# Loading the inputs of the next step one step ahead in the inner attention (8 cores)

## What is computed

```python
def _layer(x, wqkv, qs, ksc, wo, lg, lb, w1, b1, w2, b2):
    h = shift_token(x)                 # upper half of the features comes from the token before
    qkv = h @ wqkv                     # 1024 -> 3 * 512
    q, k, v = to_heads(...)            # 8 heads of 64
    q = l2norm(q) * qs;  k = l2norm(k) * ksc
    q, k = rotary_xpos(q, k)           # q*cos*scale + rotate_half(q)*sin*scale; k with 1/scale
    o = local_attention(q, k, v)       # windows of 512: own and previous, masked, softmax
    x = x + o @ wo
    ...                                # then shift, layer norm, gated feed-forward
```

## Time and profile before

| what | us |
|---|---|
| median of 3 runs (lowest, highest) | 8637.81 (8518.31, 8813.91) |
| the profiled execution | 8547.56 |
| its span, on core 6, the slowest | 8545.7 |
| spans of the 8 cores | 8432.1 to 8545.7 |

### The profile page before, as it was taken

One profiled execution on the slowest core, in us unless ns is written; L12 is line 12 of the kernel. 1 busy time (PEld: TensorE's weight loads), 2 busy tenths in 40 slices (PEclk: granted clock), 3 DMA queues, 4 the chain that ended last, 5 costly groups with the idle time before them and its releaser, 6 DMA issues. The chain is left out here.

```text
span 8545.7 us, 72782 instructions; the slowest of 8 cores (8432.1 to 8545.7 us)
## 1 busy us (share of the span) xinstructions
PE 5767.5 (67%) x21696; PEld 2068.7 (24%) x21696; DVE 2308.5 (27%) x4472; ACT 2490.9 (29%) x4771; POOL 634.1 (7%) x944
## 2 busy tenths in 40 slices
PE   1139677777777557767758877957776749779853
PEld 0013121222122112212213333412222214334321
DVE  1101221221110333334321322224333321321347
ACT  0002556666767412222211111112222221111201
POOL 0010000000000000000011111110000001111100
PEclk7568788888989866667669989966666659889876
DMA  9982001110110241121156665631112146645643
GB/s 79 86 88 73 6 25 20 30 30 7 23 25 1 47 83 35 35 59 45 35 103 95 73 105 95 83 90 35 35 39 65 35 88 80 95 98 82 87 138 138
DMA packets 694032, 531.89 MB, mean 62 GB/s; under 512 B 426620, under 2 KB 560092, under 8 KB 693664
## 3 DMA queue, kind: packets, MB, share of 16 engines
q0 software_dynamic: 472720, 208.37, 23.0%
q1 hardware_dynamic: 220944, 318.86, 15.3%
HBM read 466.56 MB, written 176.19 MB: 75 GB/s over the span
## 5 line engine op out<-in xcount | busy, mean ns | idle before, releaser
L1341 PE MATMUL p_pb<-p_hn,p_w 128*128 128x512 bf16 (+1 forms) x5632 | 1250.1, 386 | 216.1 <-DVE p_hn L1257 148.3
L600 ACT ACTIVATE p_pt<-p_pss 128x512 bf16<-128x512 f32 (+3 forms) x2304 | 1168.4, 559 | 481.8 <-PE p_pss L368 288.7
L383 PE MATMUL p_psz<-p_pt,p_v 128*65 128x512 bf16 x2304 | 777.5, 422 | 183.9 <-DVE p_zt L496 103.2
L1341 PEld LDWEIGHTS p_pb<-p_hn,p_w 128*128 128x128 bf16 (+1 forms) x5632 | 557.2, 99 | 911.6 <-issue 269.8
L368 PE MATMUL p_pss<-p_qtb,p_kt 64*128 64x512 bf16 (+3 forms) x2304 | 556.2, 404 | 234.9 <-ACT p_pt L600 219.7
L1356 PE MATMUL p_pb<-p_h,p_w 128*128 128x512 bf16 (+1 forms) x2816 | 648.4, 385 | 27.3 <-DVE p_x L1280 19.3
L810 PE MATMUL p_pb<-p_xq,p_wqkv 128*128 128x512 bf16 x1024 | 282.1, 444 | 464.3 <-DMA p_xq<-xb 406.4
L1087 ACT ACTIVATE p_pt<-p_pb 128x128 bf16<-128x128 f32 (+1 forms) x960 | 367.4, 434 | 748.9 <-PE p_pb L870 747.7
L877 PE MATMUL p_pb<-p_pt,p_vr 128*65 128x512 bf16 x960 | 501.6, 630 | 107.3 <-DVE p_pt L1003 104.3
L1308 ACT ACTIVATE p_glu<-p_pb,p_bc 128x512 bf16<-128x512 f32 x352 | 241.9, 687 | 1097.1 <-PE p_pb L1341 1097.0
L1267 DVE SCALAR_TENSOR_TENSOR p_h<-p_pb,p_bc,p_glu 128x512 bf16<-128x512 f32 x352 | 264.4, 751 | 966.2 <-PE p_pb L1341 966.2
(11 more groups left out here) (158 smaller groups left out, 5299.2 us busy)
## 6 DMA issues: line engine op xcount, KB each, us to landing
p_w<-w POOLq DMA_DIRECT2D x336, 256.0 KB, 4.2
p_xf<-xf SPq DMA_DIRECT2D x16, 2048.0 KB, 15.3
xf<-p_x POOLq DMA_DIRECT2D x128, 256.0 KB, 5.1
xb<-p_x POOLq DMA_DIRECT2D x256, 128.0 KB, 4.4
p_hf<-xf SPq DMA_DIRECT2D x32, 1024.0 KB, 9.3
p_xr<-xf SPq DMA_DIRECT2D x16, 2048.0 KB, 9.4
xf<-p_x SPq DMA_DIRECT2D x128, 256.0 KB, 2.7
xf<-p_stage SPq DMA_DIRECT2D x32, 512.0 KB, 27.5
```

The source lines that it names most:

```text
L383: t.matmul(ps_z[ZBANK[h]][0:65, 0:512], v_bf[:, kt * 520 + g * 65:kt * 520 + g * 65 + 65], pt[GS % 8][:, 0:512], start=(kt == 0), stop=(kt ...
L600: s.activation(pt[GS % 8][:, off:512], ps_s[GS % 3][:, off:512], AF.Exp, scale=0.125).then_inc(sE.sem, 1)
L1341: inst = t.matmul(pb[bank + gi % 2][0:jw, :] if jw < 128 else pb[bank + gi % 2][:, :], w1buf[:, (seq % 4) * NC * 128 + kc * jw: (seq % 4) ...
```

## The change

`xq_in` and `tabs` become twice as large, and step `tb` uses the half `tb % 2`. Each half has its own semaphore. Step 0 loads its own inputs and those of step 1. Step `tb` (1 to 6) loads those of step `tb + 1`, after two waits for semaphore values that had been reached when the step before ended; step 7 loads only `xf_cur`. The load of `xf_cur` is still that of the own step, and comes behind the others. TensorE and DVE keep their waits, on the semaphore of their half; from step 1 on the value they wait for is that at the start of the step.

```diff
-    xq_in = en(nc.sbuf_tensor("p2_xq" + L, [128, NC * 512], BF16))
+    xq_in = en(nc.sbuf_tensor("p2_xq" + L, [128, 2 * NC * 512], BF16))
-    tabs = en(nc.sbuf_tensor("p2_tab" + L, [128, 4 * 512], F32))
+    tabs = en(nc.sbuf_tensor("p2_tab" + L, [128, 2 * 4 * 512], F32))
-    lxq = Ctr.get(en_sem, nc, "p2_lxq")
+    lxq2 = [Ctr.get(en_sem, nc, f"p2_lxq{i}") for i in range(2)]
-    ltb = Ctr.get(en_sem, nc, "p2_ltb")
+    ltb2 = [Ctr.get(en_sem, nc, f"p2_ltb{i}") for i in range(2)]
...
             @blk.sync
             def _(sy):
+                def load_tb(tbl):
+                    xo = (tbl % 2) * NC * 512
+                    to = (tbl % 2) * 4 * 512
+                    sy.dma_start(xq_in[:, xo:xo + 4 * 512].rearrange("p (c j) -> p c j", c=4),
+                                 xb_in[0:512, 1 + tbl * 512:1 + (tbl + 1) * 512]
+                                 .rearrange("(c p) j -> p c j", p=128)
+                                 ).then_inc(lxq2[tbl % 2].sem, 16)
...
+                    for i, tab in enumerate([tab_cs, tab_sn, tab_ci, tab_si]):
+                        sy.dma_start(tabs[:, to + i * 512:to + (i + 1) * 512],
+                                     tab[:, tbl * 512:(tbl + 1) * 512]
+                                     ).then_inc(ltb2[tbl % 2].sem, 16)
+                    ltb2[tbl % 2].val += 64
+
+                if tb == 0:
+                    load_tb(0)
+                if tb + 1 < NQB:
+                    if tb >= 1:
+                        sy.wait_ge(tV.sem, tV0)
+                        sy.wait_ge(vQ.sem, vQ0)
+                    load_tb(tb + 1)
                 sy.dma_start(xf_cur[:, :].rearrange("p (c j) -> p c j", c=NC),
...
             @blk.tensor
             def _(t):
-                t.wait_ge(lxq.sem, lxq0 + 32)
+                xo = (tb % 2) * NC * 512
+                t.wait_ge(lxq2[tb % 2].sem, lxq20[tb % 2] + (32 if tb == 0 else 0))
...
             @blk.vector
             def _(v):
-                v.wait_ge(ltb.sem, ltb0 + 64)
+                to = (tb % 2) * 4 * 512
+                v.wait_ge(ltb2[tb % 2].sem, ltb20[tb % 2] + (64 if tb == 0 else 0))
```

More of the change, by code:

```diff
@@ L758, in _p2_inner_attn @@
             msidx[u] = mpos.get(u, 0)
-        lxq0, lxf0, ltb0 = lxq.val, lxf.val, ltb.val
+        lxf0 = lxf.val
+        lxq20 = [c.val for c in lxq2]
+        ltb20 = [c.val for c in ltb2]
         tQ0, vQ0, tV0, vV0, sSq0 = tQ.val, vQ.val, tV.val, vV.val, sSq.val
@@ L772, in _ @@
             def _(sy):
[L773 to L781, removed]
+                def load_tb(tbl):
[5 more added lines that the diff above has]
+                                 ).then_inc(lxq2[tbl % 2].sem, 16)
+                    sy.dma_start(xq_in[:, xo + 4 * 512:xo + NC * 512]
+                                 .rearrange("p (c j) -> p c j", c=4),
+                                 xb_in[512:1024, 0 + tbl * 512:0 + (tbl + 1) * 512]
+                                 .rearrange("(c p) j -> p c j", p=128)
+                                 ).then_inc(lxq2[tbl % 2].sem, 16)
+                    lxq2[tbl % 2].val += 32
+                    for i, tab in enumerate([tab_cs, tab_sn, tab_ci, tab_si]):
[10 more added lines that the diff above has]
+                    load_tb(tb + 1)
                 sy.dma_start(xf_cur[:, :].rearrange("p (c j) -> p c j", c=NC),
@@ L784, in _ @@
                              .rearrange("(c p) j -> p c j", p=128)).then_inc(lxf.sem, 16)
-                lxq.val += 32
                 lxf.val += 16
-                ltb.val += 64
             @blk.gpsimd
@@ L811, in _ @@
                                         wqkv_bf[:, kc * 1536 + mc * 128:kc * 1536 + mc * 128 + 128],
-                                        xq_in[:, kc * 512:(kc + 1) * 512],
+                                        xq_in[:, xo + kc * 512:xo + (kc + 1) * 512],
                                         start=(kc == 0), stop=(kc == NC - 1))
@@ L820, in _ @@
                         inst = t.matmul(pb[2 + tt % 2][:, :],
-                                        xq_in[:, kc * 512 + tt * 128:kc * 512 + tt * 128 + 128],
+                                        xq_in[:, xo + kc * 512 + tt * 128:
+                                              xo + kc * 512 + tt * 128 + 128],
                                         wqkv_bf[:, kc * 1536 + 1024:kc * 1536 + 1536],
@@ L932, in _ @@
             def _(v):
-                v.wait_ge(ltb.sem, ltb0 + 64)
+                to = (tb % 2) * 4 * 512
+                v.wait_ge(ltb2[tb % 2].sem, ltb20[tb % 2] + (64 if tb == 0 else 0))
                 for i in range(4):
                     v.tensor_single_scalar(ctabs[:, i * 512:(i + 1) * 512],
-                                           tabs[:, i * 512:(i + 1) * 512],
+                                           tabs[:, to + i * 512:to + (i + 1) * 512],
                                            scol[:, i:i + 1], ALU.mult).then_inc(vch.sem, 1)
```

## The result

The changed kernel took 8387.86 us (median of 10 runs, lowest 8307.37), the kernel before 8541.16 us in 10 runs beside it (lowest 8453.84). The ratio is 0.978, with a 95% interval of 0.974 to 0.982: 189 us less, where 153 were forecast and the range was 8330 to 8530. That the two medians of all runs lie 153 us apart, exactly the forecast, is chance (see the part on the prediction).

The account below looks back on a forecast made before the run. The prediction took the serial path across each attention step boundary (stores, drain, barrier, loads, projection) as the bound on that stretch. Its sum, 97 - 1 + 48 + 9 = 153 us off 8547.6, gave 8395 us, range 8330 to 8530.

Parts of the forecast that it names:

- Order of the waits: Between attention steps: stores, drain, barrier, xq and table loads, projection, all serial; one 23.23 us pause is 15.2 drain, 8.1 load.
- Term 1: TensorE's wait for xq after the release, 6.9 us in each of 14 steps, goes: gain 97 less 1 us.
- term 2: The stop ahead of the 17th matmul, where DVE waits for the tables, shrinks in 14 steps: gain 48 us.
- term 3: TensorE's clock in the projection dips less once the stop is gone: gain 9 us, bounds 0 and 20.
- What is added: Extra issues, waits, later xf_cur load and drain at the attention steps cost 0, between minus 15 and plus 15 us.
- longer drains: Rival: shifted loads and stores meet in memory, drains at step ends grow 4 us each, 56 us lost: 8450 us; chance 0.05.
- TensorE ready late: Rival: TensorE must fetch its next step's instructions after the release, leaving a 57 us gain: 8490 us; chance 0.09.
- Clock at the lower level: Rival: TensorE runs the whole projection at its slow clock, 45 us slower: 8593 us; chance 0.04.
- Clock that doesn't fall: Rival: after the shorter pause the first 16 matmuls run at full clock, 40 us more gain: 8355 us; chance 0.05.

Follow-up runs that it names:

- e1: The changed kernel run again with no edit, for a second trace: 8454 us in one run, against 8558 to 8631 us before.
- e4: The changed kernel with the inner attention's step blocks ending without POOL's drain: ratio to before 0.954 (0.937 to 0.970).
- e7: The kernel before with only xq loaded a step ahead, the own step's tables issued behind those loads: 8618 us in one run, beside 8602 and 8615 us before.
- e3: The kernel before with only the four tables loaded a step ahead: ratio to before 0.985 (0.954 to 1.015).
- e2: The kernel before with only xq loaded a step ahead, the own step's tables issued ahead of those loads: ratio to before 0.9991 (0.992 to 1.007).
- e9: The changed kernel with work left out: xq and xf loaded in step 0 alone, later steps load only tables: 8380 us in one run.
- e6: The changed kernel with the loads of the next step and of xf issued behind the first pair of heads: ratio to before 0.983 (0.967 to 1.000).

## Why the prediction was right, and where it was off

*Order of the waits.* Right: drain, release, load, tables, in this order; TensorE starts 0.3 us after the release (0.1 forecast), and the stop at the 17th matmul is gone. The pause ahead of a step came to 10.7 us (A and B in e1), under the 13 to 15 us forecast.

*Term 1, 96 us.* Measured 96 us (B from 7.1 to 0.3, 14 times).

*Terms 2 and 3, 57 us.* Measured 44 us on the mean of the cores and of two traces of before. The sum had been made on core 6 of one trace, with stops of 52.5 us; in that trace the cores' means of C lie between 17.7 and 21.4 us. In the steps of which the traces have all 64 matmul records (84 of 112 in each trace), the time from the start of the 16th to that of the 17th was 3.1 and 2.1 us before and 0.2 us in e1, 33 us in 14 steps where term 2 had 48; the stretch from the 17th matmul to v fell from 11.3 and 10.8 to 10.4 us, 10 us where term 3 had 9. So term 3 was right, and term 2 too large for the mean of the cores. On core 6 alone C fell by more, from 21.2 to 15.7 us. C came down to 15.9 us, under the 17.1 of the single step 0 on which I had built: its first 16 matmuls took 6.4 us, while in the mean of the steps the 16th starts 5.3 us after the first, before and in e1 alike.

*What is added: 0 for the drain.* This is the step that failed in size: "as bytes and their place in a step are the same". The bytes were, the drains were not, and 51 us came out of it that the sum did not have; I had kept 15 us for it, and only the loss (longer drains, 5%) as a rival. The prediction had named a sign for it: it is wrong if the drains' median moves by over 1 us, and it moved by 3.0 to 4.5. Why the drains became shorter stays open. Together 96 + 44 + 51 make 191 us against 153. Of what I had set to 0 "at worst some 5 us each" at the two steps 0, layer 0 shows a little: its C is 20.1 us in e1, against 18.3 and 18.0 before. That the median still agrees with the forecast of 8395 us to 7 us is luck: five of the ten runs took 8307 to 8339 us, three of them below the range's lower end of 8330, the other five 8437 to 8747 us, and the median of 8388 us is the middle of the gap between the two groups. The ratio came to 0.978 where 0.982 was forecast, and the interval lies on both sides of the 2% that I had set as bound.

*Rivals.* TensorE ready late: refuted by B in every run with xq loaded ahead, down to pauses of 2.1 us, and the fetch of which the Trainium skill speaks (Runtime: NRT & Kernel Launch, Instruction fetch mechanics) cost nothing at these branches. Clock at the lower level: refuted, C fell. Clock that doesn't fall: not with a pause of 10 to 15 us, and not quite with the 2.1 us of e4 either, where it fell for some 3 us behind the pause. Longer drains: the opposite.

*Additivity.* The sum was right as a sum of this change only. It treated term 1 and term 2 as two waits in a row; e7 and e3 show that term 1 alone would have been worth nothing, as the tables were on the same path behind it.

## What to carry to other kernels

When a stage waits for a store to land, then for a load, and then for a second load, one wait can hide another: work out the time at which the last of them ends with each one gone. Here taking out one of them brought between nothing (xq alone, in the old order of the queue) and 84 us (the tables), and all three 329. A drain or barrier behind stores is a transfer in disguise; here it was worth removing once the next stage had its inputs (144 us in the stage), and not before (12 us). The changed kernel without the drain beats both, at 0.954 of the time before.

## What the runs showed that was not expected

With the same 3 MB of stores a step, single drains took from 6 to 19 us, and their mean went with what the next step waits for: mean 12 us wherever DVE waits for tables of its own step (before, e2, e7), 9.6 us where only TensorE waits for xq (e3), and 8.5 to 10.9 us where no load is waited for (e1, e9, e6). Most of these are one trace each, and single cores stand out (8.5 us on core 4 of e7), so this is an order that was seen and not a cause. The fall over the steps in the changed kernel came into the theory only after e1 had been seen; the rise with later loads was in no theory of mine. The cause between the cores is open.
